# A two-layer transformer on one core: planes in the second mixture, fewer blocks, norms per batch

## The chip, the cores and the metric

The kernel runs on 1 core of a Trainium2 chip. The metric is the device time in microseconds; lower is better. The engines are TensorE (PE, with PEld for its weight loads), VectorE (DVE), ScalarE (ACT), GpSimd (POOL) and SyncE (SP), and 16 DMA engines that all queues share.

## What is computed

Input is x of 8 batches x 256 tokens x 256 features, f32. Four residual steps follow, each on a normalised x:

```python
x = x + attention(layernorm(x))            # 16 heads of 16
x = x + moe4(layernorm(x))                 # first mixture: 4 experts, hidden 512, top 2, shared expert
x = x + rwkv_time_mixing(layernorm(x))     # k, v, r products, WKV recurrence, norm, output product
x = x + moe8(layernorm(x))                 # second mixture, per token:
    logits = x @ gate_w.T + gate_b
    top_vals, top_idx = top_k(logits, 2); routing = softmax(top_vals)
    h = x @ w1[e].T + b1[e];  y = h_glu * sigmoid(1.702 * h_glu) * (h_lin + 1)
    out += routing_e * (y @ w2[e].T + b2[e])
```

A layernorm is (x - mean) / sqrt(var + 1e-5) over the 256 features.

## The kernel before

The residual x lies in SBUF for the whole run as `m.x_res`, 16 tiles (NT) of 128 tokens x 256; a batch is 2 tiles (S = 2, B = 8). The program is a string of phases. Each phase is a block in which the five engines run their own instruction lists, held together by semaphores; at its end all engines meet at a barrier, GpSimd resets the phase's semaphores, and a second barrier opens the next phase (`phase`, L1879 to L1885). `build_program` (L1864) runs attention, then `mixture_layer` for the first mixture (tag f0, 4 experts, hidden 512) with time mixing in it, then `mixture_layer` for the second (tag f1, 8 experts, hidden 256).

A mixture layer has four phases. `router_phase` (L751) normalises x with `m.mv` and `m.rstd`, writes it to DRAM (`xn_dram`) for later gathers, makes the gate's logits and splits the weights into high and low parts. `rank_phase` (L998) chooses two experts per token and sorts the 4096 (token, choice) pairs into tiles of 128 rows, each of one expert: 35 tiles in the first mixture, 39 in the second (`v.tiles`). It leaves `token_of` (which token each row of a tile gathers) and, in the first mixture only (`v.planes`), `slot_of` (where each row's result goes); in the second `row_of` (where each token finds its results).

`expert_phase` (L1149) runs over the tiles. GpSimd gathers a tile's rows from DRAM with an indirect DMA (L1205, ring of 6 buffers); TensorE transposes them, multiplies with the expert's first weights (L1272), transposes the gated product and multiplies with the second weights (L1293) into one PSUM bank, number 7, `y_psum`; ScalarE copies it to `yout`, a ring of 4 (L1335, `y_done`). TensorE's `down(t)` waits for the copy of tile t-1 (L1287).

- In the first mixture GpSimd scatters `yout` to DRAM (L1219) into two planes, the first choice of token n in row n, the second in row 2048 + n. Rows of a tile that are unused go to 128 spare rows that all tiles share, and each scatter waits for the one before (L1218). `rwkv_phase` (L1468), a phase of its own, loads the planes batch by batch with 16 plain DMAs from SyncE (L1591), ScalarE weights them and GpSimd adds them to x.
- In the second mixture SyncE stores `yout` tile by tile (L1243), and `gather_phase` (L1412) follows: per tile of 128 tokens GpSimd gathers both results (L1428), VectorE adds them with their weights (L1438), SyncE stores the output (L1450).

`rwkv_phase` orders its work by a hand-written schedule (L1499) that every engine walks. In iteration b it holds, for VectorE: scores(b), gap(b), gate(b-1), add_shift(b-1), scan(b), vary(b-1), divide(b) with `wkv` at its end (L1777), add(b-1) with the statistics of the new x (L1807), and stats(b+3) (L1730 to L1738) while there is such a batch. After the last batch VectorE aggregates the statistics of all 16 tiles (`aggregate`, L54), adds the epsilon (L1813), and GpSimd takes the power -1/2 (L1861) for the second mixture's norm.

Of the kernel before, what the change touches and what calls it, by code (L numbers as in the profile page):

```python
# [7 lines left out]
ALU = mybir.AluOpType  # L8
# [40 lines left out]


def aggregate(dve, m, aggr_done):

    for t in range(NT):
        last = dve.bn_aggr(m.mv[:, t, :], m.bn6[:, t, :])  # L54
    last.then_inc(aggr_done, 1)
    dve.wait_ge(aggr_done, 1)
# [656 lines left out]
class Mixture:  # L713

    def __init__(self, tag, experts, hidden, gated, shared, slope, lin_bias):
        self.tag, self.experts, self.hidden, self.shared = tag, experts, hidden, shared
        self.gated = gated
        self.slope = slope
        self.lin_bias = lin_bias
        self.tiles = 2 * NT + experts - 1  # L720
        self.hb = hidden // P
        self.planes = shared


def mixture_memory(nc, v, ctx):
# [6 lines left out]
    if v.planes:  # L732
        k.slot_of = sb("slot_of", [P, v.tiles], mybir.dt.uint32)
    else:
        k.row_of = sb("row_of", [P, 2 * NT], mybir.dt.uint32)
# [4 lines left out]
    k.y_dram = nc.dram_tensor(f"{v.tag}_y", [2 * TOK + P if v.planes else v.tiles * P, D], F32).ap()  # L740
# [257 lines left out]
def rank_phase(nc, m, v, k, ctx):  # L998
# [20 lines left out]
    pos_i, unused = sb("pos_i", [P, 2, NT], I32), sb("unused", [P, NTL])  # L1019
    row_oh = sb("row_oh", [P, 2 * NT, P], F16)  # L1020
# [14 lines left out]
    def _(act):  # L1035
# [3 lines left out]
        if v.planes:  # L1039
            act.wait_ge(tiles_known, 1)  # L1040
            act.activation(tile_tok[:, 0:NT, 1, :], tile_oh[:, 0:NT, :], ACT.Copy, scale=-1.0).then_inc(first_plane, 1)

    @block.tensor
    def _(pe):
# [10 lines left out]
        if v.planes:  # L1055
            pe.wait_ge(first_plane, 1)
            for j in range(NT):
                last = pe.matmul(m.banks[:, 3, 0:NTL], row_oh[:, j, :], tile_tok[:, j, 1, :],
                                 start=(j == 0), stop=(j == NT - 1))
            last.then_inc(listed, 1)  # L1060

    @block.vector
    def _(dve):
# [7 lines left out]

        source = lg
# [43 lines left out]
        if not v.planes:  # L1116
            dve.tensor_copy(k.row_of[:], posf[:].rearrange("p c t -> p (c t)"))
# [21 lines left out]
        if v.planes:  # L1139
            then(dve.scalar_tensor_tensor(out=unused[:], in0=token, scalar=0.0, in1=m.neg_row[:].broadcast_to([P, NTL]),  # L1140
                                          op0=ALU.is_equal, op1=ALU.mult))
            dve.wait_ge(listed, 3)
            then(dve.scalar_tensor_tensor(out=unused[:], in0=plane, scalar=float(TOK), in1=unused[:],
                                          op0=ALU.mult, op1=ALU.subtract))
            then(dve.scalar_tensor_tensor(out=k.slot_of[:], in0=unused[:], scalar=2.0 * TOK, in1=token,
                                          op0=ALU.add, op1=ALU.add))


def expert_phase(nc, m, v, k, ctx, A, r):  # L1149

    HB, NTL, HID = v.hb, v.tiles, v.hidden
    GB, YB = 6, 4
# [13 lines left out]
    gathered, stored = [sem(f"gathered{z}") for z in range(GB)], [sem(f"stored{z}") for z in range(YB)]  # L1166
    scattered = sem("scattered")
# [9 lines left out]
    y_psum = m.banks[:, 7, 0:D]  # L1177
# [21 lines left out]
    block = ctx.enter_context(nc.Block())  # L1199

    @block.gpsimd
    def _(pool):
# [12 lines left out]
        for t in range(NTL):  # L1215
            if v.planes:
# [6 lines left out]
        if v.planes:  # L1223
            pool.wait_ge(scattered, 16 * NTL)
# [12 lines left out]

    if not v.planes:
        @block.sync
        def _(sp):  # L1240
            for t in range(NTL):
                sp.wait_ge(y_done, t + 1)
                sp.dma_start(k.y_dram.rearrange("(t p) d -> p t d", p=P)[:, t, :], yout[:, t % YB, :]).then_inc(stored[t % YB], 16)  # L1243
            for z in range(YB):
                sp.wait_ge(stored[z], 16 * ((NTL - z + YB - 1) // YB))

    @block.tensor
    def _(pe):
        class PE:
# [33 lines left out]
            def down(self, t):  # L1283
# [3 lines left out]
                at_least(pe, y_done, t)  # L1287
                ht = (ht_hi, ht_lo)
                if v.lin_bias:
                    pe.matmul(y_psum, m.ones_r[:], k.b2[:, e, :], start=True, stop=False)  # L1290
                steps = [(hb, c, a) for hb in range(HB) for c in range(2) for a in range(2 - c)]
                for i, (hb, c, a) in enumerate(steps):
                    last = pe.matmul(y_psum, ht[a][:, t % 2, hb * P:(hb + 1) * P], k.w2[c][hb][:, e, :],  # L1293
# [6 lines left out]
    def _(act):  # L1300
        class Act:
# [27 lines left out]
            def down(self, t):  # L1329
                act.wait_ge(down_done, t + 1)  # L1330
                if v.planes:
                    at_least(act, scattered, 16 * (t - YB + 1))
                elif t >= YB:
                    act.wait_ge(stored[t % YB], 16 * (t // YB))
                act.activation(yout[:, t % YB, :], y_psum, ACT.Copy).then_inc(y_done, 1)  # L1335
# [74 lines left out]


def gather_phase(nc, m, v, k, out, ctx):  # L1412

    GB = 4
    sb = lambda name, shape, dt=F32: ctx.enter_context(nc.sbuf_tensor(f"{v.tag}c_{name}", shape, dt))
    sem = lambda name: nc.alloc_semaphore(f"{v.tag}c_{name}")
    y = sb("y", [P, GB, 2, D])
    gathered = [[sem(f"gathered{z}{c}") for c in range(2)] for z in range(GB)]
    one_added, both_added, stored = (
# [526 lines left out]
```

## Time and profile before

| | us |
|---|---|
| median of 3 runs | 853.4 (853.35 to 854.92) |
| the profiled execution | 852.91 |
| its span, first to last instruction | 851.2 |

| engine | busy us | share |
|---|---|---|
| PE | 649.4 | 76% |
| DVE | 541.4 | 64% |
| ACT | 342.6 | 40% |
| POOL | 327.1 | 38% |

The stages, in us from the start of the span: attention to about 171, first router to 237, first ranking to 256.5, first expert block to 447.3, time mixing to 618.9, second router to 663.5, second ranking to 684.7, second expert block to 806, gather phase to the end. Busy shares are means over stages with different limits. A row of the timeline gives start, duration, engine, line, operation, output and inputs, a count if several are merged, and in brackets how long the engine was idle before and what ended that.

### The profile page before, as it was taken

The numbers are of one execution on the slowest core, as the hardware profiler recorded it, in microseconds if no ns is written. First come the engines' busy times: TensorE is split into PE (matmuls) and PEld (weight loads), VectorE is DVE, ScalarE is ACT, GpSimd is POOL, SyncE is SP. The second block draws the span as 40 slices with busy tenths as digits, with TensorE's granted clock in tenths as the row PEclk, the third lists the DMA queues.
The fourth block names the chain that finished last, engine by engine and source line by source line (L and its number), as shares of the span: only waits on it lengthen the run. The fifth ranks groups of instructions, "written<-read, shape, count | busy, mean of one in ns | idle before, by whom it ended". The sixth has DMA issues, their size and how long they took to land. (4 is left out here: it accounts for less than half of the span.)

```text
span 851.2 us, 14119 instructions
## 1 busy us (share of the span) xinstructions
PE 649.4 (76%) x4265; PEld 534.9 (63%) x4265; DVE 541.4 (64%) x1122; ACT 342.6 (40%) x760; POOL 327.1 (38%) x306
## 2 busy tenths in 40 slices
PE   4989999669916999999944899999344069999600
PEld 3656665358815888888833788888344048888400
DVE  4578989626782556444421799998556748888433
ACT  1567777324402333333315566544045025555200
POOL 5877764000003343434314466634310043331075
PEclk9999999969967999999986999999755569999855
DMA  4000000045303111111106000000059023332154
GB/s 124 1 2 1 2 2 2 3 149 189 95 1 87 52 56 57 57 57 50 50 25 198 1 1 1 2 0 1 0 180 307 8 67 98 99 100 81 50 152 138
DMA packets 38466, 54.23 MB, mean 64 GB/s; under 512 B 7252, under 2 KB 30422, under 8 KB 38262
## 3 DMA queue, kind: packets, MB, share of 16 engines
q1 hardware_dynamic: 31624, 34.80, 12.7%
q0 software_dynamic: 6768, 18.49, 7.3%
q8 instruction: 41, 0.67, 0.3%
q14 instruction: 33, 0.27, 0.1%
HBM read 37.28 MB, written 15.99 MB: 63 GB/s over the span
## 5 line engine op out<-in xcount | busy, mean ns | idle before, releaser
L1611 PE MATMUL banks<-r_xt,r_w_mixed 128*128 128x256 f32 x384 | 86.6, 385 | 1.4 <-ACT r_xt L1679 1.4
L1611 PEld LDWEIGHTS banks<-r_xt,r_w_mixed 128*128 128x128 f32 x384 | 73.1, 192 | 12.4 <-ACT r_xt L1679 2.1
L1357 DVE SCALAR_TENSOR_TENSOR f0x_s<-f0x_th,banks 128x512 f32<-128x512 f32 x35 | 24.1, 689 | 82.7 <-ACT f0x_th L1316 78.0
L1219 POOL DMA_INDIRECT f_y<-f0x_yout,f_slot_of x35 | 34.4, 983 | 102.1 <-ACT f0x_yout L1335 99.9
L1205 POOL DMA_INDIRECT f1x_xg<-f_xn,f_token_of x39 | 37.0, 948 | 75.5 <-PE banks L1256 50.9
L568 DVE TENSOR_REDUCE a_ssum<-a_e 128x6 f32<-128x1536 f32 x32 | 56.0, 1749 | 2.7 <-ACT a_e L454 2.5
L1272 PE MATMUL banks<-f_w_hi,f0x_xt_hi 128*128 x140 | 56.1, 401 | 0.2 <-issue 0.2
L1316 ACT ACTIVATE f0x_th<-banks 128x512 f32<-128x512 f32 x35 | 20.9, 598 | 86.5 <-PE banks L1272 86.5
L1272 PE MATMUL banks<-f_w_hi,f0x_xt_lo 128*128 x140 | 55.6, 397 | 0.0
L1272 PE MATMUL banks<-f_w_lo,f0x_xt_hi 128*128 x140 | 55.3, 395 | 0.0
L454 ACT ACTIVATE a_e<-banks 128x1536 f32<-128x1536 f32 x32 | 46.5, 1455 | 15.8 <-PE banks L351 15.8
L663 POOL TENSOR_TENSOR a_rr<-a_ms_eps,neg_half 128x32 f32<-128x32 f32 (+1 forms) x9 | 44.0, 4890 | 20.2 <-DVE a_ms_eps L536 20.2
L1205 POOL DMA_INDIRECT f0x_xg<-f_xn,f_token_of x35 | 33.9, 969 | 30.6 <-POOLq L1885 20.2
L1428 POOL DMA_INDIRECT f1c_y<-f_y,f_row_of x32 | 30.2, 945 | 39.3 <-PEq L1882 29.9
L1293 PE MATMUL banks<-f_w_hi,f0x_ht_hi 128*128 x140 | 42.3, 302 | 0.7 <-ACT f0x_yout L1335 0.7
L351 PE MATMUL banks<-a_ut,a_qt 32*128 32x256 f32 x512 | 39.1, 422 | 3.3 <-ACT a_e L444 1.5
L1293 PE MATMUL banks<-f_w_lo,f0x_ht_hi 128*128 x140 | 39.4, 282 | 0.0
L1293 PE MATMUL banks<-f_w_hi,f0x_ht_lo 128*128 x140 | 39.4, 281 | 0.0
L1438 DVE SCALAR_TENSOR_TENSOR x_res<-f1c_y,f_weight,x_res 128x256 f32<-128x256 f32 x32 | 15.5, 485 | 33.2 <-DMA f1c_y<-f_y,f_row_of 31.1
L376 PE MATMUL banks<-a_e,a_vv 128*32 128x256 f32 x512 | 35.1, 393 | 1.9 <-DVE a_vv L583 1.8
L351 PEld LDWEIGHTS banks<-a_ut,a_qt 32*128 32x128 f32 x512 | 24.7, 196 | 18.1 <-ACT a_e L444 8.1
L1369 DVE TENSOR_TENSOR f1x_hb<-banks,f_b 128x512 f32<-128x512 f32 x39 | 27.0, 692 | 11.9 <-PE banks L1272 7.2
(330 smaller groups left out, 1889.0 us busy)
## 6 DMA issues: line engine op xcount, KB each, us to landing
f_y<-f1x_yout SPq DMA_DIRECT2D x39, 128.0 KB
f0r_stage<-in_f_w13T SPq DMA_DIRECT2D x4, 1024.0 KB
r_y<-f_y SPq DMA_DIRECT2D x16, 256.0 KB, 6.0
f1r_stage<-in_f_w13T SPq DMA_DIRECT2D x8, 512.0 KB
f0r_stage<-in_f_w2T SPq DMA_DIRECT2D x4, 512.0 KB
f_xn<-f0r_xn SPq DMA_DIRECT2D x8, 256.0 KB
f1r_stage<-in_f_w2T SPq DMA_DIRECT2D x8, 256.0 KB
f_xn<-f1r_xn SPq DMA_DIRECT2D x8, 256.0 KB
```

What stands on the lines that cost most here:

```text
L351: last = pe.matmul(scores[:, i, s, :], qt[rows, b % 2, e, k, s * P:(s + 1) * P], ut[rows, b % 2, k, :], start=True, stop=True)
L376: last = pe.matmul(av(n)[32 * i:32 * i + 32, :], values[:, b % 2, head, :, :].rearrange("p r d -> p (r d)"), side[:, S * i + s, :], start= ...
L454: act.activation(ebuf[:, n % 3, 0:SUMS_ON_DVE, :], scores[:, 0:SUMS_ON_DVE // S].rearrange("p i s t -> p (i s) t"), ACT.Exp).then_inc(exp_ ...
L568: dve.tensor_reduce(ssum[:, b % 2, NB * p:NB * p + SUMS_ON_DVE], ebuf[:, n % 3, 0:SUMS_ON_DVE, :], AX_X, ALU.add).then_inc(sum_done, 1)
L663: pool.tensor_tensor(part(rr[:]), part(ms_eps[:]), part(m.neg_half[:, 0:S * NH]), ALU.pow).then_inc(rr_found, 1)
L1205: pool.indirect_dma_start(xg[:, t % GB, :], None, k.xn_dram, bass.IndirectOffsetOnAxis(ap=k.token_of[:, t:t + 1], axis=0)).then_inc(gather ...
L1219: pool.indirect_dma_start(k.y_dram, bass.IndirectOffsetOnAxis(ap=k.slot_of[:, t:t + 1], axis=0), yout[:, t % YB, :], None).then_inc(scatte ...
L1272: last = pe.matmul(out, xt[a][:, t % 2, kb * P:(kb + 1) * P], k.w13[c][kb][:, e, cols], start=(i == 0), stop=(i == len(steps) - 1))
L1293: last = pe.matmul(y_psum, ht[a][:, t % 2, hb * P:(hb + 1) * P], k.w2[c][hb][:, e, :], start=(i == 0 and not v.lin_bias), stop=(i == len(s ...
L1369: dve.tensor_tensor(hb1[:, t % 2, :], up_banks(t), k.b1[:, e, :].rearrange("p e n -> p (e n)"), ALU.add).then_inc(hb1_done, 1)
L1428: pool.indirect_dma_start(y[:, t % GB, c, :], None, k.y_dram, bass.IndirectOffsetOnAxis(ap=k.row_of[:, c * NT + t:c * NT + t + 1], axis=0) ...
L1611: last = pe.matmul(bank(1 + kind)[:, eb * T:(eb + 1) * T], r.w_mixed[:, kind, j // KB, j % KB, eb * P:(eb + 1) * P], xt[:, b % 2, j % KB, ...
```

## The change

- The second mixture uses planes as well: `rank_phase` computes `slot_of` there (an extra ScalarE copy, 16 TensorE products, three VectorE operations), no `row_of`. GpSimd scatters its results; SyncE's stores and `gather_phase` are gone. In their place `planes_phase`, in the same block as the experts, loads the planes with 8 DMAs of 256 KB from SyncE (plane 0) and 8 from ScalarE (plane 1), VectorE adds them batch by batch, SyncE stores the output per batch.
- Unused rows go to spare rows of each tile's own (`neg_spare`), scatters no longer wait for one another; each ring slot of `yout`, now 8, has its own semaphore. On GpSimd the scatter of tile t-3 stands behind the gather of tile t+6.
- Results of the second mixture go to PSUM banks 7 and 3 in turn, those of the first stay in bank 7.
- Time mixing runs in the first expert block: no barrier between them, SyncE waits for the scatters' semaphores before its loads.
- The aggregate, the epsilon and the power for the next norm are taken per batch in a step `level`: level(b-2) stands before add(b-1). GpSimd drains once, after batch 2's additions.

```diff
@@ expert_phase
-    GB, YB = 6, 4
+    GB, YB, SCATTER_LAG = 6, 8, 3
-    y_psum = m.banks[:, 7, 0:D]
+    y_banks = (7, 3) if U == 1 else (7,)
+    y_psum = lambda t: m.banks[:, y_banks[t % len(y_banks)], 0:D]
@@ GpSimd
-        for t in range(NTL):
-            if v.planes:
-                pool.wait_ge(y_done, t + 1)
-                at_least(pool, scattered, 16 * t)
-                pool.indirect_dma_start(k.y_dram, bass.IndirectOffsetOnAxis(ap=k.slot_of[:, t:t + 1], axis=0),
-                                        yout[:, t % YB, :], None).then_inc(scattered, 16)
+        for t in range(NTL + SCATTER_LAG):
             if t + GB < NTL:
                 gather(t + GB)
+            if t >= SCATTER_LAG:
+                done = t - SCATTER_LAG
+                pool.wait_ge(y_done, done + 1)
+                pool.indirect_dma_start(k.y_dram, bass.IndirectOffsetOnAxis(ap=k.slot_of[:, done:done + 1], axis=0),
+                                        yout[:, done % YB, :], None).then_inc(scattered[done % YB], 16)
@@ TensorE
-                at_least(pe, y_done, t)
+                at_least(pe, y_done, t + 1 - len(y_banks))
@@ planes_phase, new, in place of gather_phase
+    def all_scattered(eng):
+        for semaphore, value in zip(k.scattered, k.scatters):
+            eng.wait_ge(semaphore, value)
+    @block.scalar
+    def _(act):
+        all_scattered(act)
+        for b in range(B):
+            act.dma_start(y[:, 1, S * b:S * b + S, :], rows(k.y_dram[TOK:2 * TOK], b)).then_inc(here[1][b], 16)
+    @block.vector
+    def _(dve):
+        for b in range(B):
+            for c, added_to in ((0, first_added), (1, added)):
+                dve.wait_ge(here[c][b], 16)
+                if c == 1:
+                    dve.wait_ge(first_added, b + 1)
+                for t in range(S * b, S * b + S):
+                    x_t = m.x_res[:, t, :]
+                    last = dve.scalar_tensor_tensor(out=x_t, in0=y[:, c, t, :], scalar=k.weight[:, c, t:t + 1], in1=x_t,
+                                                    op0=ALU.mult, op1=ALU.add)
+                last.then_inc(added_to, 1)
+    @block.sync
+    def _(sp):
+        all_scattered(sp)
+        for b in range(B):
+            sp.dma_start(y[:, 0, S * b:S * b + S, :], rows(k.y_dram[0:TOK], b)).then_inc(here[0][b], 16)
+        for b in range(B):
+            sp.wait_ge(added, b + 1)
+            sp.dma_start(rows(out, b), m.x_res[:, S * b:S * b + S, :]).then_inc(stored, 16)
+        sp.wait_ge(stored, 16 * B)
@@ rwkv_phase, schedule and steps
+            if b > 1:
+                w.level(b - 2)
             if b > 0:
                 w.add(b - 1)
@@
+            def level(self, b):                     # VectorE
+                dve.wait_ge(done["bn_done"], b + 1)
+                for t in range(S * b, S * b + S):
+                    last = dve.bn_aggr(m.mv[:, t, :], m.bn6[:, t, :])
+                last.then_inc(done["aggr_done"], 1)
+                dve.wait_ge(done["aggr_done"], b + 1)
+                dve.tensor_scalar(m.var_eps[:, two], m.mv[:, two, 1], LN_EPS, None, ALU.add).then_inc(done["eps_done"], 1)
@@
+            def level(self, b):                     # GpSimd
+                pool.wait_ge(done["eps_done"], b + 1)
+                pool.tensor_tensor(m.rstd[:, two], m.var_eps[:, two], m.neg_half[:, 0:S], ALU.pow).then_inc(done["next_rstd"], 1)
@@ GpSimd, gather_up
                 pool.tensor_tensor(two, two, y[:, 1, S * b:S * b + S, :], ALU.add).then_inc(done["added"], 1)
+                if b == 2:
+                    pool.drain()
```

## Rows read from the trace of the kernel before

**Rows 1.** Windows by stage: stretch, length, busy time (instructions) by engine, clock, DMA.
```profile
core 0: us, PE busy (x) PEld busy (x) DVE busy (x) ACT busy (x) POOL busy (x), PEclk, DMA share, GB/s
684.70:806.00 121.30, 109.82 (x663) 93.42 (x663) 86.50 (x195) 54.28 (x157) 36.99 (x39) 0.94 0.28 86
806.00:851.20 45.20, 0.00 (x0) 0.00 (x0) 15.51 (x32) 0.00 (x0) 30.23 (x32) 0.50 0.49 140
```

**Rows 2.** Timeline, end of the second expert block (PE, ACT) and what follows (POOL).
```profile
800.25 0.58 PE L1290 MATMUL banks<-f_b,ones_r 128*128 x1 [0.67 <-ACT f1x_yout L1335]
...
802.14 0.38 ACT L1335 ACTIVATE f1x_yout<-banks 128x256 f32<-128x256 f32 x1 [2.14 <-PE banks L1293]
806.03 0.94 POOL L1428 DMA_INDIRECT f1c_y<-f_y,f_row_of  x1 [29.90 <-PEq L1882]
```

**Rows 3.** Timeline, from the last results of the first mixture to time mixing.
```profile
434.24 0.38 ACT L1335 ACTIVATE f0x_yout<-banks 128x256 f32<-128x256 f32 x1 [0.84 <-PE banks L1293]
...
434.95 0.96 POOL L1219 DMA_INDIRECT f_y<-f0x_yout,f_slot_of  x1 [2.18 <-ACT f0x_yout L1335]
...
436.58 0.38 ACT L1335 ACTIVATE f0x_yout<-banks 128x256 f32<-128x256 f32 x1 [1.96 <-PE banks L1293]
438.09 0.96 POOL L1219 DMA_INDIRECT f_y<-f0x_yout,f_slot_of  x1 [2.19 <-DMA f_y<-f0x_yout,f_slot_of]
447.28 9.30 SPq L1591 DMA_DIRECT2D r_y<-f_y  x16
...
449.95 0.91 ACT L1664 ACTIVATE r_y<-r_y,f_weight 128x256 f32<-128x256 f32 x2 [1.38 <-DMA r_y<-f_y]
```

**Rows 4.** Time mixing loop: one window (columns as in rows 1), then VectorE's timeline.
```profile
533.00:550.00 17.00, 17.00 (x86) 14.83 (x85) 16.01 (x26) 9.96 (x18) 10.42 (x10) 1.00 0.00 1
...
551.12 0.96 DVE L1777 TENSOR_TENSOR r_wkv<-r_num,r_rden 128x512 f32<-128x512 f32 x1
...
554.34 0.25 DVE L1734 BATCH_NORM_AGGREGATE mv<-bn 128x2 f32<-128x6 f32 x2
...
554.70 0.16 DVE L1738 TENSOR_SCALAR r_ve_in<-mv 128x2 f32<-128x2 f32 x1
...
568.13 0.69 DVE L1777 TENSOR_TENSOR r_wkv<-r_num,r_rden 128x512 f32<-128x512 f32 x1
...
585.28 0.69 DVE L1777 TENSOR_TENSOR r_wkv<-r_num,r_rden 128x512 f32<-128x512 f32 x1
```

**Rows 5.** Timeline, end of time mixing and the second router's first instruction.
```profile
610.54 0.71 POOL L1846 TENSOR_TENSOR r_rstd<-r_ve,neg_half 128x2 f32<-128x2 f32 x1 [9.63 <-DVE r_ve L1794]
...
613.39 1.17 DVE L54 BATCH_NORM_AGGREGATE mv<-bn 128x2 f32<-128x6 f32 x16
...
614.84 2.90 POOL L1861 TENSOR_TENSOR rstd<-var_eps,neg_half 128x16 f32<-128x16 f32 x1 [3.60 <-DVE var_eps L1813]
...
618.90 0.30 POOL L868 MEMSET f1r_spare<- 1x256 f32 x1 [1.16 <-POOLq L1885]
```

**Rows 6.** Timeline of GpSimd: its first product in the time mixing loop.
```profile
473.44 1.27 POOL L1837 TENSOR_TENSOR r_sc<-r_sc,r_vs 128x512 f32<-128x512 f32 x1 [9.84 <-ACT r_sc L1709]
```

**Rows 7.** Timeline of VectorE: the end of the first mixture's ranking.
```profile
254.69 0.19 DVE L1138 TENSOR_SCALAR f_token_of<-banks 128x35 uint32<-128x35 f32 x1 [0.33 <-PE banks L1052]
...
255.40 0.19 DVE L1145 SCALAR_TENSOR_TENSOR f_slot_of<-f0k_unused,banks 128x35 uint32<-128x35 f32 x1
```

**Rows 8.** Timeline of GpSimd in the steady part of either expert block.
```profile
312.71 0.96 POOL L1205 DMA_INDIRECT f0x_xg<-f_xn,f_token_of  x1 [0.30 <-issue]
...
705.38 0.94 POOL L1205 DMA_INDIRECT f1x_xg<-f_xn,f_token_of  x1 [1.72 <-PE banks L1256]
```

**Rows 9.** Window of time mixing's plane loads, columns as in rows 1.
```profile
447.28:461.80 14.52, 3.77 (x10) 2.88 (x11) 2.48 (x12) 8.81 (x18) 7.77 (x12) 0.50 0.91 290
```

**Rows 10.** The tail: VectorE's additions as a group of lines, then the last one.
```profile
L1438 DVE SCALAR_TENSOR_TENSOR x_res<-f1c_y,f_weight,x_res 128x256 f32<-128x256 f32 x32 | 15.5, 485 | 33.2 <-DMA f1c_y<-f_y,f_row_of 31.1 <-issue 2.1
...
847.73 0.48 DVE L1438 SCALAR_TENSOR_TENSOR x_res<-f1c_y,f_weight,x_res 128x256 f32<-128x256 f32 x1 [0.84 <-DMA f1c_y<-f_y,f_row_of]
```

More of the change, by code:

```diff
@@ L48, in split_product @@
     return last
[L51 to L56, printed above, removed]
 class Names:
@@ L1054, in _ @@
         last.then_inc(listed, 1)
[L1055 to L1060, printed above, removed]
+        pe.wait_ge(first_plane, 1)
+        for j in range(NT):
+            last = pe.matmul(m.banks[:, 3, 0:NTL], row_oh[:, j, :], tile_tok[:, j, 1, :],
+                             start=(j == 0), stop=(j == NT - 1))
+        last.then_inc(listed, 1)
     @block.vector
@@ L1070, in then @@
             dve.wait_ge(step, done[0])
+        dve.tensor_scalar(neg_spare[:], m.count_up[:, 0:NTL], -float(P), m.neg_row[:, 0:1], ALU.mult, ALU.add)
         source = lg
@@ L1138, in _, with expert_phase @@
         then(dve.tensor_scalar(k.token_of[:], token, float(TOK), None, ALU.add))
[L1139 to L1149, printed above, removed]
+        then(dve.scalar_tensor_tensor(out=unused[:], in0=token, scalar=0.0, in1=neg_spare[:],
+                                      op0=ALU.is_equal, op1=ALU.mult))
+        dve.wait_ge(listed, 3)
+        then(dve.scalar_tensor_tensor(out=unused[:], in0=plane, scalar=float(TOK), in1=unused[:],
+                                      op0=ALU.mult, op1=ALU.subtract))
+        then(dve.scalar_tensor_tensor(out=k.slot_of[:], in0=unused[:], scalar=2.0 * TOK, in1=token,
+                                      op0=ALU.add, op1=ALU.add))
+def expert_phase(nc, m, v, k, ctx, block, A, r):
     HB, NTL, HID = v.hb, v.tiles, v.hidden
-    GB, YB = 6, 4
+    GB, YB, SCATTER_LAG = 6, 8, 3
     sb = lambda name, shape, dt=F32: ctx.enter_context(nc.sbuf_tensor(f"{v.tag}x_{name}", shape, dt))
@@ L1236, in _ @@
             sp.wait_ge(r_loaded, 16 * 11)
[L1238 to L1245, printed above, removed]
     @block.tensor
@@ L1465, in rwkv_memory, with rwkv_phase @@
     return r
-def rwkv_phase(nc, m, r, k, ctx):
+def rwkv_phase(nc, m, r, k, ctx, block):
     EB = KB
@@ L1555, in schedule @@
                 w.stats(b + 3)
-        for step in (w.centre, w.square, w.gate, w.shift, w.add_shift, w.project, w.deviate, w.vary, w.add):
+        for step in (w.centre, w.square, w.gate, w.shift, w.add_shift, w.project, w.deviate, w.vary):
             step(B - 1)
+        w.level(B - 2)
+        w.add(B - 1)
+        w.level(B - 1)
     class Work:
@@ L1582, in add, with level @@
         def add(self, b): pass
-    block = ctx.enter_context(nc.Block())
+        def level(self, b): pass
     @block.sync
     def _(sp):
+        for semaphore, value in zip(k.scattered, k.scatters):
+            sp.wait_ge(semaphore, value)
         for b in range(B):
```

102 lines of the change are left out of this document (33 added, 69 removed).

## The prediction

> **What bounds the kernel now.** I read the profile in this order: the stages in time, then each place where one stage hands over to the next, then the steady loops between them. The kernel is a string of stages, and no engine is full over the whole span, so every edit is priced in the stage where it stands.
>
> The last stage is the one to see first. From 806.0 to 851.2 us TensorE does nothing, the DMA engines are half busy (0.49), and GpSimd issues 32 gathers; in the second expert stage before it TensorE is busy 109.8 of 121.3 us [rows 1]. The last result of the second mixture is copied at 802.14 + 0.38 = 802.52, so 851.2 - 802.5 = 48.7 us pass with no matmul at all [rows 1, 2]. The same kind of hole follows the first mixture: its last result is ready at 436.96, its last scatter is issued at 438.09, and the first load of time mixing at 447.28, 10.3 us after that result [rows 3]. The time mixing loop is the opposite: per batch about 17.1 us, with TensorE busy all of 17.0 and VectorE 16.0 of them [rows 4].
>
> **The change part by part.**
>
> *Hand-over behind the first mixture.* Before: result ready 436.96, scatter 438.09 (it waited for the scatter before it), block end, semaphore reset, barrier, first load 447.28. After: the scatter need not wait for its predecessor, and SyncE waits for the scatters' own semaphores in the same block. A scatter follows its result by 0.33 us (434.62 to 434.95), and the one of 434.95 had landed by 438.09, at most 3.14 later [rows 3]. So the first load goes out at 436.96 + 0.33 + 3.14 + 0.1 (my allowance for SyncE to wake) = 440.5 instead of 447.3: 6.8 us saved. The ScalarE table load moves into the wait, where it costs nothing: even now ScalarE's first weighing begins at 449.95, when its data land, 2.67 after the load's issue [rows 3]. What lies in the old gap is not fully shown. With the landing at 441.2 about 6 us are left for block end and reset, while the same two steps behind time mixing take 1.16 us [rows 3, 5]. Either GpSimd is slow to come to rest behind its own DMAs (then the 5 us extra vanish, as GpSimd's rest is no longer waited for), or the last scatter lands late (then they stay and only about 1.9 are saved: 1.16 and the 0.8 of earlier issue). I take 6.8, since the scatter before it landed in time; ends 1.9 and 7.0. The added GpSimd drain in batch 2 sits where GpSimd idles 9.84 us up to 473.44 [rows 6]; it may take the 5 us there for nothing. Without that cover it would cost the 5.
>
> *Per-batch norms.* Gone at the end: 14 of 16 aggregates and the wide power. Now the last add is followed by 1.17 us of aggregates, the small add and a 2.90 us power, up to 617.74 [rows 5]. After: two aggregates (0.25 [rows 4]), 0.28 for the small add and its hand-over, a 0.71 power as for the other 128x2 ones; from 613.39 that ends at 614.63: 3.1 saved. Added in the loop on VectorE: two aggregates and one small operation, 0.36 us (554.34 to 554.70), for each of batches 0 to 5 [rows 4]. Three of these fall in iterations 2 to 4, where VectorE also takes statistics of batch b+3. There the product waits for nothing between 551.12 and 568.13 but its own queue, so all three count: +1.1 (ends 0 and 1.3). For iterations 5 to 7 the period is no shorter than before although those statistics are gone (568.13 to 585.28 is 17.15), so TensorE sets it and the 0.36 is hidden [rows 4]. Batch 6 fits in VectorE's wait for the last root. On GpSimd the eight 0.7 us powers lie in its idle time.
>
> *Ranking.* In the second mixture VectorE computes slots: in the first, token list to slot list takes 255.40 - 254.69 = 0.71 us, TensorE's extra products and ScalarE's copy lying beside it [rows 7]. The new row offsets are one small operation at the start of each ranking, 0.1 each by the 0.08 between two such starts in rows 4. Together +0.9.
>
> *Second expert loop.* SyncE's stores become GpSimd scatters. GpSimd now issues one gather per tile and idles 1.72 of 2.67 us; a scatter of 0.96 and an issue gap of 0.30 is 1.26 us, leaving 0.46 idle [rows 3, 8]. The lag of three lets gathers run ahead: GpSimd queues behind a wait for a result only a scatter, and a gather six tiles ahead. So nothing here. Two result banks in turn: TensorE waits for the copy only once, 0.67 us before the last tile [rows 2]; in the loop it is full. Saved 0.65. The last tile's matmuls run slower behind that wait (granted clock down); if the clock holds, under 1 us more is won. I leave that out of the sum.
>
> In the Trainium skill, SBUF — State Buffer, section "SBUF: two separate sides", there is a rule against this move: DMAs issued from GpSimd have their descriptors written through a port pair that VectorE can lock, so such a DMA can look blocked, and it advises SyncE or ScalarE queues. Here the gather takes 0.94 us beside a VectorE that is busy 86.5 of the stage's 121.3 us [rows 1, 8], so the trace speaks against a large effect; by the rule the scatter could be several times longer (rival 3).
>
> *The tail.* Before: 48.7 us from the last result. After, with t0 as the first plane load: t0 = result + 0.33 + 3.14 + 0.1 = +3.6. What moves is 4.2 MB in and 2.1 MB out. The same 4.2 MB load exists: time mixing's y, sixteen 256 KB loads, 14.5 us at 0.91 of the DMA engines and 290 GB/s, start included [rows 9]. So the loads end by t0 + 14.5. The stores share SyncE's ring behind plane 0's loads; seven of them, 1.8 MB at the same rate, are out at t0 + 20.8. VectorE: 32 additions of 0.485 us, 15.5 in all [rows 10], from t0 + 3.3 (two loads must land, first one 2.67 [rows 3]) to t0 + 18.8 at most, less when they follow back to back; then the last store, 3.0 us as behind the last addition now (848.21 to 851.2) [rows 10], plus 0.35 for twice the size: t0 + 22. That is later by little; as the additions should be less than 0.485 apart back to back, I take t0 + 21.6, so result + 25.2. Saved 48.7 - 25.2 = 23.5. No row shows loads issued by ScalarE or loads and stores so mixed: ends 18 (the traffic at 250 GB/s) and 26 (additions at 0.42, loads never late).
>
> **Sum.** 6.8 + 3.1 - 1.1 - 0.9 + 0.65 + 23.5 = 32.0 us. The profiled execution took 852.9 us with a span of 851.2; that makes 820.9. The median shown, 853.4, is 0.5 above it, so 821.4; I say 821.
>
> **The rivals.**
> 1. *The 5 us behind the first mixture stay* (landing, not the barrier, or the drain exposed). For: nothing shows which. Against: the scatter before landed in 3.14. Price 5: 826.
> 2. *The tail is bound by mixed traffic.* Loads and stores slow each other, the additions wait for loads. For: the present tail, which mixes both, only moves 140 GB/s [rows 1]; against: that is paced by gather issue. Price 5.5: 826.5. The Trainium skill's DMA: Bandwidth & Descriptors, "Queues, rings and completion order", has an engine alternate between queues packet by packet, so ScalarE's loads would compete with SyncE's stores rather than precede them; that is a share of this price.
> 3. *Slower than before: GpSimd becomes the bound of the second expert loop.* Each tile then costs what gather and scatter cost. To eat 32 us in 39 tiles it needs 0.83 us per tile beyond the 0.46 idle, a scatter of about 2.25 us instead of 0.96. Between these, partial: scatter of 1.6 us costs 0.2 x 39 = 7 us. For: VectorE's two-input operations are dense there. Against: 0.94 and 0.96 us beside a busy VectorE in both loops [rows 3, 8]. Full price 855 and more.
> 4. *The change doesn't do what it says*, that is, hardly any tail is saved, because the last scatter is far behind its tile. GpSimd's 0.46 us of idle per tile says it is not; 840.
>
> **How the numbers follow.** Forecast as summed 0.72, rival 1 0.11, rival 2 0.10, rival 3 at full price 0.02 and rival 4 or partial rival 3 0.05. The bounds: best is 821 less 2.5 (tail), 1.1 (norms), 0.9 (clock), some 816; I allow 815. The other end takes in rivals 1 and 2, 828. A difference of 0.2% (1.7 us) is about what a measurement of this kernel can tell from no change; all but rival 3 lie far beyond it on the faster side: faster 0.97, same 0.01, slower 0.02.
>
> **What would show it.** First load of time mixing some 3.6 us after the last result of the first mixture, and a GpSimd gap in its batch 2. Loop periods of 17.5 in iterations 2 to 4 and 17.1 behind them. Router start about 2 us behind the last aggregates. GpSimd in the second expert loop: pairs of 0.95, small idle, tile period 2.66 unchanged. Last result to end: 25 us. The prediction is wrong if the tile period grows, if the first loads wait 8 us or more, or if the DMA engines in the tail stay under 250 GB/s.

## The result and the profile after

The changed kernel took 844.35 us (median of 4 runs, 841.46 to 845.94) against 853.38 us (4 runs) before: a ratio of 0.989, 95% interval 0.9858 to 0.9922. Faster, as forecast, but by 9 us and not by 32, and outside the range of 815 to 828. The profiled execution took 843.94 us with a span of 842.1.

The same kernel was timed again later, among the experiments, and took 820.5 us there (4 runs, 819.74 to 821.79; before: 849.26; ratio 0.9647, interval 0.9594 to 0.970). Both figures are real, and most of what follows is about what lies between them. I call a group of kernels that ran one after the other on one chip a set; set 0 is that of the result, sets 1 to 5 those of the experiments.

The last stage and the one before it, in set 0, as rows of the windows view; these answer to [rows 1]:

```profile
core 0: us, PE busy (x) PEld busy (x) DVE busy (x) ACT busy (x) POOL busy (x), PEclk, DMA share, GB/s
697.80:818.00 120.20, 104.59 (x619) 87.49 (x618) 80.66 (x182) 49.78 (x147) 67.23 (x67) 0.96 0.24 73
818.00:842.10 24.10, 0.00 (x0) 0.00 (x0) 13.46 (x32) 0.00 (x0) 0.97 (x1) 0.55 0.83 272
```

The tail went from 48.7 to 24.1 us and the DMA engines in it from half busy to 0.83. But the second expert loop, from its first to its last result, takes 119.8 us where it took 101.15. The second group of the profile's view by tile, of the tile that holds the results (duration, first and last start), in set 0 and then in set 3:

```profile
L1308 ACT ACTIVATE f1x_yout<-banks x39: 365/377/386, 697.8 to 817.6; 128x256 f32<-128x256 f32 x39
L1206 POOL DMA_INDIRECT f_y<-f1x_yout,f_slot_of x39: 965/988/1212, 698.5 to 818.3; - x39
```

```profile
L1308 ACT ACTIVATE f1x_yout<-banks x39: 367/377/385, 694.2 to 793.6; 128x256 f32<-128x256 f32 x39
L1206 POOL DMA_INDIRECT f_y<-f1x_yout,f_slot_of x39: 969/987/1217, 694.9 to 794.3; - x39
```

The same 39 results and 39 scatters of the same length, in 119.8 us and in 99.4. All six stretches between events that both kernels have, in us, from one profile each:

| from the event above to | before | after, set 0 | after, set 3 | forecast of the change |
|---|---|---|---|---|
| last result of mixture 1 (copy starts) | 436.6 | 435.9 | 434.7 | 0 |
| first weighted value of time mixing (r_wkv) | 46.5 | 39.7 | 39.4 | -6.8 |
| last small add of the next norms | 131.5 | 136.3 | 136.2 | +0.2 |
| first result of mixture 2 | 86.4 | 86.0 | 83.9 | -1.3 |
| last result of mixture 2 | 101.15 | 119.8 | 99.4 | -0.65 |
| end | 49.05 | 24.5 | 24.5 | -23.5 |
| span | 851.2 | 842.1 | 818.1 | -32.0 |

(The end of time mixing is split over two rows: of the 3.1 us forecast there, 0.9 lie ahead of the small add and 2.2, the power, behind it.) Set 3 gives -33.1 for a forecast of -32.0, but against the profile of before from set 0; by the medians of set 3 alone (849.26 and 820.5 us) the change brought 28.8 us. Set 0 differs from set 3 by 20.4 us in one row and by at most 2.1 in any other.

What happens in that row. Timeline of set 0 near 718 us, only ScalarE, GpSimd and the instructions that they and VectorE wait for (start, duration, engine; in brackets idle time before it):

```profile
715.60 0.38 ACT L1308 ACTIVATE f1x_yout<-banks 128x256 f32<-128x256 f32 x1
...
715.71 1.02 POOL L1190 DMA_INDIRECT f1x_xg<-f_xn,f_token_of  x1 [0.30 <-issue]
...
716.50 0.38 PE L1256 MATMUL banks<-ident,f1x_h 128*128 128x128 f32 x2
...
717.04 0.99 POOL L1206 DMA_INDIRECT f_y<-f1x_yout,f_slot_of  x1 [0.30 <-issue]
...
718.33 0.97 POOL L1190 DMA_INDIRECT f1x_xg<-f_xn,f_token_of  x1 [0.30 <-issue]
...
719.12 0.69 DVE L1342 TENSOR_TENSOR f1x_hb<-banks,f_b 128x512 f32<-128x512 f32 x1 [2.44 <-DMA f_xn<-f1r_xn]
720.43 0.38 ACT L1301 ACTIVATE f1x_ht_hi<-banks 128x256 fp32r<-128x256 f32 x1 [4.46 <-remote]
```

ScalarE's copy at 720.43 needs the two transposes that TensorE started at 716.50, and nothing else that is not older. It starts 3.5 us after their end. In the undisturbed loop it follows at once (set 3):

```profile
784.97 0.38 ACT L1308 ACTIVATE f1x_yout<-banks 128x256 f32<-128x256 f32 x1
...
785.62 0.97 POOL L1206 DMA_INDIRECT f_y<-f1x_yout,f_slot_of  x1 [1.64 <-ACT f1x_yout L1308]
...
786.37 0.39 ACT L1301 ACTIVATE f1x_ht_hi<-banks 128x256 fp32r<-128x256 f32 x1 [1.03 <-PE banks L1256]
```

The trace also has the times at which semaphores were raised. Beside the ends of the instructions that raise them:

```
TensorE instruction (line)          its end    semaphore raised   late
product into the hidden bank (1248)  716.67        718.99          2.32
transposes of h (1256)               716.89        720.41          3.52
transposes of x (1232)               717.11        720.46          3.35
product into the result bank (1269)  717.94        720.54          2.60
product into the hidden bank (1248)  719.33        720.62          1.29
```

So TensorE's rows go on at full pace to 719.3 while its signals are held up and then come in a burst of four within 0.2 us; then everyone catches up, TensorE idle for 2.8 us. Such pauses cost clock as well: the two transposes took 0.38 us at 716.50 and 0.69 at 722.12, behind the pause. The granted clock of the loop was 0.96 in set 0 and 1.00 in set 3, and TensorE was busy 104.6 us for the work that took it 98.0 there: 6.6 of the 20.4 us. In the second expert loop of set 0, 44 of TensorE's 143 recorded signals come over 0.5 us late, up to 3.8; of VectorE's and ScalarE's none that was recorded does. In set 3 none of 156 is late. I call these late signals. (Fewer were recorded in set 0. In such a set the profile loses records also where no signal is late: of TensorE's 133 signals in the first mixture's loop it kept 85 in set 0 and 129 in set 3. Whether the profiling itself has a part in the late signals is not shown: every time on record of the changed kernel comes with a span and a granted clock, and none is known to stand without a profile.) The Trainium skill's Perfetto Trace Analysis, section "Tensor Engine Instruction (MATMUL, LD_WEIGHTS)", says how that can look so: a row of TensorE ends where a model puts it, and the semaphore is pushed later, when PSUM has acknowledged the write. The trace agrees in so far as the two times differ, here by up to 3.8 us.

### The profile page after: what moved, and what is told of

Same layout as the page of the kernel before. It is cut to its first block and busy times, and to the rows that moved or that the text cites. A ratio compares the mean times of both kernels' runs of the same rounds, so it can differ in the third digit from the quotient of the medians.

```text
span 842.1 us, 14068 instructions
## 1 busy us (share of the span) xinstructions
PE 658.5 (78%) x4281; PEld 539.2 (64%) x4281; DVE 543.8 (65%) x1133; ACT 343.9 (41%) x761; POOL 340.5 (40%) x320
## 3 DMA queue, kind: packets, MB, share of 16 engines
q1 hardware_dynamic: 28056, 31.79, 11.8%
## 5 line engine op out<-in xcount | busy, mean ns | idle before, releaser
L1206 POOL DMA_INDIRECT f_y<-f1x_yout,f_slot_of x39 | 38.9, 997 | 47.8 <-ACT f1x_yout L1308 43.0
L1190 POOL DMA_INDIRECT f1x_xg<-f_xn,f_token_of x39 | 38.9, 997 | 34.2 <-POOLq L1879 22.6
L655 POOL TENSOR_TENSOR a_rr<-a_ms_eps,neg_half 128x32 f32<-128x32 f32 (+1 forms) x9 | 44.0, 4891 | 17.5 <-DVE a_ms_eps L528 17.5
L1190 POOL DMA_INDIRECT f0x_xg<-f_xn,f_token_of x35 | 34.0, 973 | 33.2 <-POOLq L1879 20.4
L1269 PE MATMUL banks<-f_w_lo,f0x_ht_hi 128*128 x140 | 39.4, 282 | 0.0
L1269 PE MATMUL banks<-f_w_hi,f0x_ht_lo 128*128 x140 | 39.4, 281 | 0.0
L1301 ACT ACTIVATE f1x_ht_hi<-banks 128x256 fp32r<-128x256 f32 x39 | 15.0, 384 | 48.8 <-PE banks L1256 31.1
```

The source lines that it names most:

```text
L655: pool.tensor_tensor(part(rr[:]), part(ms_eps[:]), part(m.neg_half[:, 0:S * NH]), ALU.pow).then_inc(rr_found, 1)
L1190: pool.indirect_dma_start(xg[:, t % GB, :], None, k.xn_dram, bass.IndirectOffsetOnAxis(ap=k.token_of[:, t:t + 1], axis=0)).then_inc(gather ...
L1269: last = pe.matmul(y_psum(t), ht[a][:, t % 2, hb * P:(hb + 1) * P], k.w2[c][hb][:, e, :], start=(i == 0 and not v.lin_bias), stop=(i == le ...
```

## The experiments

Theory A: late signals come when GpSimd issues DMAs densely. Each of its DMAs takes 0.95 to 1.0 us and a 0.3 us gap; the changed loop has two per tile of 2.66 us, the loop before had one, the first mixture's loop two per 4.83 us. The trace of before had a hint that I had not looked for: three late signals (up to 1.66 us) at 699.5, just behind ten gathers back to back, ahead of the first result.

### Set 1: whose fault it is

**Results stored by SyncE.** The second mixture's scatter replaced by a plain store of the tile; the last stage loads the same amount from there, so that the kernel leaves out the placing of results by token:

```
-  pool.wait_ge(y_done, done + 1); pool.indirect_dma_start(k.y_dram, <slots of tile>, yout[...])
+  sp.wait_ge(y_done, t + 1); sp.dma_start(k.y_dram[2 * TOK + t * P:...], yout[...])
```

> The changed kernel, but the second mixture's results are stored by SyncE in the order of the tiles, as before the change, instead of scattered by GpSimd; the last stage then loads the same amount from there, so that the placing of the results by token is left out and the output is not the reference's. Two result banks stay. Theory A (GpSimd issuing a gather and a scatter per tile of 2.66 us makes TensorE's signals come late): the stretch from the first to the last result of the second mixture falls from 119.8 back to about 101 us, no late signals, total about 825. Theory B (the second result bank, or anything else that this kernel keeps): the stretch stays near 120 and the total near 844.

```profile
L1317 ACT ACTIVATE f1x_yout<-banks x39: 367/376/383, 696.3 to 795.5; 128x256 f32<-128x256 f32 x39
```

820.75 us (820.29 to 823.09, 4 runs), ratio 0.964 (0.9609 to 0.967); the stretch is 99.2 us with no late signal in it, and three just ahead of it, as before the change. The same bytes move, so the amount of traffic is not the cause, and the loss hangs on the scatters that GpSimd issues. The edit changes two things at once, though: the issuing engine, and the kind of DMA, from an indirect scatter to a plain store in smaller packets (0.9 KB in the mean, 2.7 for the indirect ones). No run has plain DMAs issued by GpSimd.

**One result bank.** `y_banks = (7,)`.

> The changed kernel with one result bank in the second mixture (bank 7 alone) as before the change. Theory A: the stretch stays near 120 us (119 to 122), total 844 to 846. Theory B (alternating between banks 7 and 3 disturbs TensorE): the stretch falls to about 101 us, total about 826.

Stretch 116.35 us, 62 late signals, 836.3 us in all. The banks are not the cause. (The stretch missed its 119 to 122 us, and the total its 844 to 846, because the loop also began 4.2 us earlier in this run, and was 3.4 us shorter.)

**GpSimd busy, but not with DMAs.** As the first, with a multiplication on GpSimd in the scatter's place:

```
+  pool.tensor_tensor(idle_work[:], idle_work[:], idle_work[:], ALU.mult)
```

> As the kernel with SyncE's stores in the second mixture (results not placed by token, output not the reference's), but GpSimd computes a 128x256 multiplication of some 0.9 us where it issued each scatter, so that it is as busy as in the changed kernel. Theory A (it is the DMA issue): stretch about 101 us, total about 825. Rival C (a GpSimd that is busy at all, or its SBUF port, holds up the loop): stretch 110 us or more, total 834 or more.

```profile
L1212 POOL TENSOR_TENSOR f1x_idle_work<-f1x_idle_work 128x256 f32<-128x256 f32 x39 | 29.2, 750 | 40.9 <-ACT f1x_yout L1323 40.9
```

The multiplication took 0.75 us, somewhat less than I meant; stretch 99.1 us, three late signals ahead of it, 821.3 us. A busy GpSimd is no harm; rival C falls.

**One more gather per tile in the first mixture**, where nothing was late:

```
+  if r: pool.indirect_dma_start(again[:], None, k.xn_dram, <tokens of the tile>)
```

> The changed kernel with one more gather per tile in the first mixture's loop, into a buffer that nobody reads, issued right behind the scatter: GpSimd then issues three DMAs in a tile of 4.83 us (3.8 us of it taken) where it issued two. Theory A (the density of GpSimd's DMA issue, wherever it stands): late TensorE signals appear in the first mixture too, which show none now, and its loop grows by 5 to 20 us. Rival (the cause is particular to the second mixture): the first mixture's loop keeps its 4.83 us per tile, total 844.

```profile
L1316 ACT ACTIVATE f0x_yout<-banks x35: 383/384/405, 275.7 to 442.3; 128x256 f32<-128x256 f32 x35
```

The loop grew from 159.7 to 166.6 us, with 48 late signals where there had been none. So it is no matter of the second mixture: three GpSimd DMAs per 4.83 us bring it on in another loop. (This kernel's second loop, unchanged, took 117.3 us, and the whole 851.8.)

### Set 2: smaller rates, and a surprise

**Half of the scatters.** GpSimd scatters even tiles, SyncE stores the odd ones (twice, so that more bytes move than in the changed kernel, 104 GB/s against 74 in set 5). The placing of results by token is left out here too.

> In the second mixture GpSimd scatters the results of even tiles only; SyncE stores those of odd tiles, twice (once more in place of the even tile before it), so that as many bytes move; the last stage loads from SyncE's copies, so the placing by token is left out of the output, which is not the reference's. GpSimd then issues 1.5 DMAs per tile (0.56 per us at 2.66 us a tile), between the 1 and the 2 measured. Theory A with a threshold (late TensorE signals only when GpSimd issues nearly without pause): stretch from first to last result 99 to 103 us, hardly any late signals. Theory A in proportion to the scatters: half of the growth, 108 to 112 us. If the transfers themselves, not GpSimd's issue, were the cause, e1 had already shown it; this run has the same bytes.

**Norms moved** out of the iterations in which GpSimd adds:

```
-  if b > 1:
-      w.level(b - 2)
+  if b > 4:
+      w.level(2 * (b - 5))
+      w.level(2 * (b - 5) + 1)
```

> The changed kernel with the norms of batches 0 to 5 taken in the last three iterations of the time mixing loop (two batches in each) instead of one iteration each from iteration 2 on. Theory (in iterations 2 to 4 the small add beside GpSimd's addition costs VectorE 0.96 us instead of 0.17 and the loop is bound by VectorE there): periods of iterations 2 to 4 fall from about 18.1 to 17.1 us, those of 5 to 7 stay at 17.1 to 17.2 as VectorE has room; the stage is 3 us shorter. Rival (the period is set by something else): 18.1 stays.

**Gathers spread**, 16 tiles ahead:

```
-  if t + GB < NTL: gather(t + GB)
+  for g in range(gather_at(t), min(gather_at(t + 1), NTL)): gather(g)   # 23 over 35 tiles, GB = 16
```

> The changed kernel, with the whole computation, but the second mixture's gathers run 16 tiles ahead instead of 6 (the buffers double as one plane of the last stage) and those left for the loop, 23 for 36 tiles, are spread evenly, so that GpSimd issues 1.64 DMAs per tile in the loop instead of 2. Theory A: the stretch falls from 119.8 to between 103 and 113 us and the total to 829 to 839, lower if the half-scatter run shows no growth at all. Rival (not the rate, but each scatter costs its share): stretch 118 or more, total 843.

**Both.**

> The spread gathers and the moved norms together: 2 to 3 us below the kernel with the spread gathers alone; if both theories hold, 826 to 837 us.

Measured: 820.88, 820.06, 821.17 (816.63 to 823.88) and 817.72 us (815.95 to 818.6), with stretches of 99.35, 99.28, 99.44 and 99.26 us and not one late signal in any. The norms kernel was the surprise: its second expert loop is that of the changed kernel, two GpSimd DMAs per tile, and it is 20 us shorter than in set 0.

```profile
L1308 ACT ACTIVATE f1x_yout<-banks x39: 365/376/383, 694.4 to 793.7; 128x256 f32<-128x256 f32 x39
L1206 POOL DMA_INDIRECT f_y<-f1x_yout,f_slot_of x39: 969/987/1215, 695.1 to 794.4; - x39
```

Either moving the norms cured it (hard to see how, 100 us earlier) or the set did not have it. The spread gathers (103 to 113 expected) and both together (826 to 837 us in all) missed what was expected of them. The runs of this set say nothing on rates.

### Set 3: the changed kernel beside its variants

> The changed kernel as it is, once more. In the set of runs before this one four variants that leave GpSimd's 1.5 to 2 DMAs per tile in place all had a second expert loop of 99.3 us without one late TensorE signal, one of them (the moved norms) with nothing changed in that loop. They ran on another chip than the first set. Theory X (the late signals belong to a chip, or to its state at the time, as well as to the rate): this kernel too gives a stretch of 99.3 us and about 823 us on the one chip, and about 120 and 844 on the other; whichever this set falls on, the kernels of this set agree with it. Theory Y (the variants of the second set removed the cause, by a shift of timing or place): this kernel gives 844 beside variants that give 820 on the same chip.

> The moved norms once more, beside the changed kernel on one chip. X: the same second expert loop as the changed kernel beside it (both 99 or both near 120), and 2 to 3 us less in all. Y: 99.3 us beside 120 of the changed kernel.

> The gathers spread, 16 tiles ahead, beside the changed kernel on one chip. X on a chip with late signals: 1.64 DMAs per tile instead of 2, so a stretch between 103 and 115 us; on one without: 99.4. Y: 99.4 beside 120.

> The extra gather per tile in the first mixture's loop, beside the changed kernel on one chip. It lengthened that loop by 6.9 us with 48 late signals in the first set. X: the same on a chip where the changed kernel has late signals; on one without, the first mixture's loop keeps its 159.7 to 160 us and no signal is late. Y: 6.9 us longer wherever it runs.

820.5 (4 runs), 819.02, 822.66 and 825.38 us; stretches 99.4, 99.3, 99.3 and 99.3; no late signal, not with the dense gathers in the first mixture either, whose loop took 160.06 us there. The moved norms gave 1.5 us in all, for 2 to 3 expected, from one run. Theory Y falls. What decides is the rate together with something of the set.

### Sets 4 and 5: is it the chip, and is it the rate

Set 1 was on one chip, set 2 on another, set 3 on a third; sets 4 and 5 fell on the chip of set 2.

> Whole computation, gathers 16 tiles ahead and spread, norms moved. On a chip without late signals: stretch 99.3 us, about 818. On one with them (told by the semaphore records of TensorE, of which the profile there also keeps fewer: some 93 instead of 138 in the first mixture): if the rate of GpSimd's DMAs decides, 103 to 115 us in the stretch and 820 to 834 in all, against 120 and 844 of the changed kernel there; if the chip alone decides, about 118 and 840.

> Half of the second mixture's scatters, the rest stored by SyncE (the placing by token left out of the output, which is not the reference's). On a chip without late signals: 99.4 us and 821 as before. On one with them: with a threshold in the rate 99 to 103 us; in proportion to the scatters 108 to 112 us.

Both had late signals, on the chip that had had none two sets earlier: 112.3 us with 39, and 107.9 us with 34; 838.28 and 830.32 us in all. The first total lies above the 820 to 834 expected. So it is not the chip but the time. The last set put the three rates side by side:

> The changed kernel beside its variants. The last set showed late signals on a chip that had shown none before, so they belong to the time of the set, not to the chip. In a set with late signals: stretch 117 to 121 us, about 844. In one without: 99.3 and 820.5.

> Half of the scatters by GpSimd, the rest stored by SyncE (placing left out of the output). In a set with late signals, if the rate sets the loss: 107 to 110 us in the stretch, clearly below the changed kernel beside it. In one without: 99.4.

> Whole computation, gathers spread, norms moved. In a set with late signals, if the rate sets the loss: 110 to 114 us, between the two beside it, and 5 to 10 us less in all than the changed kernel. In one without: 99.3 and 818.

The windows of the loop in the changed kernel, in the one with half of the scatters, and in the one with spread gathers, all of set 5:

```profile
698.00:818.00 120.00, 104.16 (x618) 87.32 (x618) 80.68 (x182) 49.66 (x147) 66.88 (x67) 0.96 0.24 74
```

```profile
695.00:804.00 109.00, 100.57 (x620) 83.65 (x618) 80.11 (x182) 48.40 (x147) 47.21 (x48) 1.00 0.34 104
```

```profile
701.00:817.50 116.50, 103.81 (x618) 86.73 (x618) 80.74 (x183) 49.61 (x147) 58.12 (x59) 0.96 0.21 67
```

The totals were 844.25, 829.57 and 843.9 us. The half-scatter kernel moves the most bytes (104 GB/s, DMA share 0.34) and loses the least; GpSimd's 67, 59 and 48 instructions go with 119.9, 116.3 and 108.5 us. Over all sets with late signals:

| GpSimd DMAs per tile, loop | stretch, us (set) | late signals from the first gather on | first gather to first result, us |
|---|---|---|---|
| 1, mixture 2 | 99.2 (1), 101.15 (before) | 3, 3, all ahead of the first result | 15.6, 15.5 |
| 1.5, mixture 2 | 107.9 (4), 108.5 (5) | 34, 43 | 15.1, 15.2 |
| 1.64, mixture 2 | 112.3 (4), 116.3 (5) | 39, 42 | 25.5, 26.1 |
| 2, mixture 2 | 119.8 (0), 117.3 (1), 119.9 (5), 116.35 (1, one bank) | 44, 45, 42, 62 | 15.7, 15.6, 15.7, 15.6 |
| 2 of 4.83 us, mixture 1 | 159.7 (0), 159.9 (5) | 0, 0 | |
| 3 of 4.83 us, mixture 1 | 166.6 (1) | 48 | |

The order is as expected, the sizes only in part: the half-scatter kernel fell inside its 107 to 110 us, the spread gathers outside their 110 to 114 in set 5, and of the 5 to 10 us less in all that I expected of them there 0.35 came.

The last column shows where the rest went. In sets 2 and 3 it is 14.6 to 14.8 us for every kernel. With the gathers 16 tiles ahead GpSimd issues 18 of them without a pause before the first result, and in a set with late signals that costs 11 us ahead of the loop. Set 5:

```profile
688.76 0.28 PE L1270 MATMUL banks<-f_w_lo,f1x_ht_hi 128*128 x1
...
690.04 0.40 PE L1249 MATMUL banks<-f_w_lo,f1x_xt_hi 128*128 x1
...
696.31 0.95 POOL L1191 DMA_INDIRECT f1x_xg<-f_xn,f_token_of  x1 [0.30 <-issue]
...
700.18 0.38 ACT L1302 ACTIVATE f1x_ht_hi<-banks 128x256 fp32r<-128x256 f32 x1 [13.33 <-remote]
...
701.87 0.69 PE L1257 MATMUL banks<-ident,f1x_h 128*128 128x128 f32 x2 [11.43 <-DVE f1x_h L1335]
```

Transposes that end at 687.99 raise their semaphore at 700.16, 12.2 us late, and TensorE stands for 11.4 us. All but one of the late signals recorded there come only when the row of gathers has ended, from 700.16 on for an end at 697.26 (in set 4 from 697.88 on for 696.48). No scatter is issued in that time, so scatters are not needed for it: gathers without a pause do the same. The same kernel in set 2 issues the same gathers and has no late signal (14.6 us). Half of the scatters, which does not lengthen that row, is the weaker dose; spreading the gathers this way is no cure.

## Why the prediction was right or wrong

**Hand-over behind the first mixture, -6.8: right.** The stretch lost 6.8 us in set 0 and 7.1 in set 3. The first load goes out 2.85 us behind the last result's end (436.23 to 439.08), for 3.6 forecast and 10.3 before [rows 3]:

```profile
435.85 0.38 ACT L1308 ACTIVATE f0x_yout<-banks 128x256 f32<-128x256 f32 x1 [1.97 <-PE banks L1269]
...
436.25 1.28 ACT L1703 ACT_TABLE_LOAD   x1
...
436.50 0.97 POOL L1206 DMA_INDIRECT f_y<-f0x_yout,f_slot_of  x1 [1.38 <-ACT f0x_yout L1308]
...
439.08 4.21 SPq L1574 DMA_DIRECT2D r_y<-f_y  x8
```

The table load lies in the wait, as said. So the last scatter had landed in time, and the 5 us were not its landing (rival 1 falls). Of the drain in batch 2 nothing shows: GpSimd's idle time ahead of its next product is 10.2 to 10.3 us, where it was 9.84 [rows 6].

**Per-batch norms, -3.1 + 1.1: the end right, the loop three times too cheap.** At the end the last aggregates start at 611.55 and the power ends at 612.78, 1.23 us, where it took 4.35 [rows 5]: 3.1 saved. In the loop I had taken 0.36 us for each batch from rows where GpSimd was quiet. The timeline of VectorE and GpSimd in iteration 4:

```profile
547.28 0.96 DVE L1760 TENSOR_TENSOR r_wkv<-r_num,r_rden 128x512 f32<-128x512 f32 x1
...
547.77 1.60 POOL L1813 TENSOR_TENSOR x_res<-x_res,r_y 128x512 f32<-128x512 f32 x1
...
548.16 0.23 DVE L1797 BATCH_NORM_AGGREGATE mv<-bn 128x2 f32<-128x6 f32 x2
548.43 0.96 DVE L1800 TENSOR_SCALAR var_eps<-mv 128x2 f32<-128x2 f32 x1
549.31 0.86 DVE L1785 SCALAR_TENSOR_TENSOR x_res<-banks,r_rstd,x_res 128x256 f32<-128x256 f32 x2
```

Two numbers per partition take 0.96 us, until GpSimd's addition ends at 549.37; in the next iteration, without that addition, the same instruction takes 0.17. The Trainium skill's SBUF — State Buffer, section "SBUF: two separate sides", tells of the port pair that VectorE and GpSimd lock against each other; here it is VectorE that waits, by 0.8 us, three times. The periods of iterations 2 to 4 came to 18.14, 18.14 and 18.15 us (17.5 forecast), those behind them to 17.16 as forecast. The moved norms bring them to 16.99, 17.16 and 17.01 (set 3), 3.3 us less than the changed kernel beside them: the cause is shown. A further 1.6 us in iteration 1 goes with the clock: TensorE's granted clock was 0.90 over the 16.7 us before it (1.00 before the change, at the same work), and the moved norms leave it there (18.76). Another 0.8 us lies between the last product and the last small add. It comes and goes with the first: in the runs of one result bank, of half the scatters in set 2, of the spread gathers in set 2 and of both edits together in sets 4 and 5 the clock stays at 1.00 in that stretch, iteration 1 takes 17.2 us, and the last part 11.7 to 11.8 us at a granted clock of 0.79; in all others 18.7 to 18.9 us, and 12.7 to 13.0 at 0.75 or 0.76. What brings the clock down in one run and not in the next is open. So time mixing gave +4.8 in set 0 (4.7 in set 3) for +0.2.

**Ranking +0.9, together with the power's part -1.3: about right** (-0.4 and -2.5 in two sets; the clock at the router's start moves this stretch by that much).

**Second expert loop, 0 - 0.65: this step failed.** The tile period, forecast unchanged at 2.66 us and named as a sign of being wrong, grew to 3.15. I summed GpSimd's time per tile, 0.94 + 0.30 + 0.96 + 0.30 of 2.67, and concluded that what is left idle hides it: "So nothing here." The sum was right: gather and scatter took 0.98 to 1.0 us, GpSimd waited 43 us for results even in set 0. What was missing is a cost that falls on another engine: issued at that density, in sets 0, 1, 4 and 5 the DMAs went with TensorE signals up to 3.9 us late in this loop, +18.6 us in set 0. Rival 3 had the place (GpSimd in this loop) and a small chance, but the wrong mechanism; it watched the scatter's own length, which never reached 1.25 us. Nor did it come as by the rule of the Trainium skill, SBUF — State Buffer, section "SBUF: two separate sides", cited in the prediction, by which VectorE holds up the descriptor writing of such a DMA: the longest scatter took 1.21 us in set 0 and 1.22 in set 3. In sets 2 and 3 the step was right: 99.4 us, 1.8 better than before, with the granted clock at 1.00.

**The tail, -23.5: right.** 24.15 us from the last result (817.95) to the end for 25.2 forecast. The first loads go out at +2.9 (3.6 forecast), the first addition starts at 824.52, the last ends 14.29 us later, the last store 3.3 behind it. No rival of mixed traffic shows:

```profile
820.83 4.13 SPq L1423 DMA_DIRECT2D f1c_y<-f_y  x8
...
824.52 14.29 DVE L1415 SCALAR_TENSOR_TENSOR x_res<-f1c_y,f_weight,x_res 128x256 f32<-128x256 f32 x32 [8.28 <-DMA f1c_y<-f_y]
...
826.41 12.80 SPq L1426 DMA_DIRECT2D out_x<-x_res  x8
```

An addition takes 0.42 us (13.46 for 32), my lower end.

So the sum of 32 us is about what the change brings where no signal is late (820.5 us for 821 forecast; 28.8 us by the medians of set 3), and 18.6 of it were taken back in set 0. That 820.5 meets 821 so closely is in part luck: the row of time mixing was forecast 4.5 us too cheap, and against that stand 1.9 us ahead of the first mixture's first result, where the change touches nothing, and 0.3 to 1.2 in each of the four other rows. Storing through SyncE instead, which removes the density and keeps the time of the rest of the change (the results are not placed by token), showed the same in a set with late signals: 820.75 us.

Of whole computations the fastest was the one with spread gathers and moved norms: 817.72 us in set 2, ratio 0.96 (0.9563 to 0.9636), 3.5 us below the spread gathers alone in the same set, and about 3 below the changed kernel of set 3. With late signals it took 838.28 and 843.9 us, the second 0.35 us below the changed kernel beside it: what the loop gains goes into the row of gathers ahead of it.

**Still open:** what the sets with late signals have in common. It was four of six, on at least two chips, one of which had both kinds; the kernel before took 851.0 to 853.4 us in them and 849.3 and 851.0 in the others, so its time hardly tells them apart. Its profile does, as every kernel's: of TensorE's 133 signals in the first mixture's loop 83 to 115 were recorded in the four sets (90 before the change), 129 in the two others. Nor is it shown what holds the signals up, only that GpSimd's indirect DMAs, neither its arithmetic nor the bytes, decide how often. Three rivals stand untested: that it is the indirect kind of DMA and not GpSimd as the issuer; that the profiling, which loses records in just these sets, has a part in it; and, as a row of TensorE ends where a model puts it, that it is the writes of the products and not the signals alone that come late.

## What to carry to other kernels

When work moves to an engine with room, its own busy time is only the first of the costs: ask also what each of its instructions does to the others, and look in the trace of before for a spot where it already runs as densely as it will (here ten gathers back to back, and three late signals behind them). Count GpSimd's DMAs per us: up to 0.41 cost nothing in either loop in any set, 0.56 and more cost 4 to 20% of a loop bound by TensorE in some, and 18 without a pause stopped TensorE for 10 to 11 us there. So don't run GpSimd's gathers far ahead in one row either. Before a forecast or a verdict on such a change, time it in more than one set, since one set alone would have called this change a gain of 1% or of 3.5%, and price a small VectorE instruction from a row that stands beside the same GpSimd instruction that it will stand beside.

## What the runs showed of the hardware

- TensorE's semaphore signals can come up to 3.9 us behind the end of its rows in a loop with two GpSimd DMAs per 2.66 us, and up to 12.2 us behind it beside 18 gathers without a pause, several signals at once. In the two expert loops they did so in four of six sets and only where GpSimd issued 0.56 or more DMAs per us (or ten and more without a pause); of VectorE's and ScalarE's recorded signals none did.
- The same program on the same chip had none of it in one set and 39 late signals in a later one (stretches of 99.3 and 112.3 us for the spread gathers with moved norms, 99.35 and 107.9 for half of the scatters).
- A one-input VectorE instruction of 128x2 elements took 0.96 us instead of 0.17 beside a two-input GpSimd addition of 128x512.
- Sixteen 256 KB loads issued by SyncE and ScalarE together with eight 256 KB stores moved 272 GB/s over the whole tail of 24.1 us.
